# Attention plus quantised feed-forward layer on eight cores: the P·V products of a head pair issued after the fourth score block, two quantisation steps moved into the loop, and one absolute-maximum reduction per group in place of two

## The reference

```python
x = L0_attn_x                                   # (8, 2048, 1024), f32
# causal attention, 16 heads of 64, no output projection
ln = _layernorm(x)
q, k, v = ln @ W_query, ln @ W_key, ln @ W_value
weights = softmax(where(causal, q @ k.T, -inf) / sqrt(64))
x = x + weights @ v
# feed-forward with ternary weights and 8-bit activations
def act_quant(x):                               # one scale per token
    scale = 127.0 / clip(max(abs(x), axis=-1), 1e-05)
    return clip(round(x * scale), -128, 127) / scale
def weight_quant(w):                            # one scale per matrix
    scale = 1.0 / clip(mean(abs(w)), 1e-05)
    return clip(round(w * scale), -1, 1) / scale
h = act_quant(_layernorm(x)) @ weight_quant(w1).T        # 1024 -> 4096
h = silu(depthwise_conv1d(h, conv_w, width 3) + conv_b)
return x + act_quant(h) @ weight_quant(w2).T             # 4096 -> 1024
```

## Time and profile before

| | us |
|---|---|
| median of the runs | 2214.39 |
| the two runs | 2199.25, 2229.52 |
| the profiled execution | 2193.41 |
| its span on the slowest core (core 5), first to last instruction | 2191.9 |
| spans of the eight cores | 2180.6 to 2191.9 |
| DVE busy | 1063.7 |
| TensorE busy | 1093.1 |
| ACT busy | 830.4 |
| GpSimd busy | 280.9 |

### The profile page before, as it was taken

One profiled execution on the slowest core, in us unless ns is written; L12 is line 12 of the kernel. 1 busy time (PEld: TensorE's weight loads), 2 busy tenths in 40 slices (PEclk: granted clock), 3 DMA queues, 4 the chain that ended last, 5 costly groups with the idle time before them and its releaser, 6 DMA issues.

```text
span 2191.9 us, 23798 instructions; the slowest of 8 cores (2180.6 to 2191.9 us)
## 1 busy us (share of the span) xinstructions
PE 1093.1 (50%) x7038; PEld 598.7 (27%) x7038; DVE 1063.7 (49%) x2058; ACT 830.4 (38%) x904; POOL 280.9 (13%) x255
## 2 busy tenths in 40 slices
PE   0577974344554455510424365373473553757465
PEld 0233421122222233200222233232232332434322
DVE  1444343523355555544546446445465464555650
ACT  3100002877755566701332432424413425242422
POOL 0000000000000000000013113113131131322220
PEclk9988985555565566655666687686686877879787
DMA  7310021753343464357322223203222232132300
GB/s 233 96 39 20 1 77 38 237 205 132 138 139 121 138 199 131 129 168 227 113 68 77 70 66 125 68 33 112 74 71 87 68 121 62 58 126 67 116 20 19
DMA packets 108273, 224.03 MB, mean 102 GB/s; under 512 B 4593, under 2 KB 70258, under 8 KB 104050
## 3 DMA queue, kind: packets, MB, share of 16 engines
q1 hardware_dynamic: 94962, 172.18, 24.5%
q0 software_dynamic: 13184, 50.34, 6.5%
HBM read 188.94 MB, written 33.55 MB: 102 GB/s over the span
## 4 chain that ended last, share of the span: by engine, by line
DVE 30%; PE 24%; DMA 17%; ACT 15%; issue 9%; DVEq 1%; POOL 1%; SPq 1%; ACTq 0%; POOLq 0%
PE psO L75 10%; PE psQK L75 7%; DMA wbuf<-w1t 6%; DVE t1s L75 5%; DVE hsil L75 4%; ACT PT L75 4%; DVE smalls L75 4%; DVE tmpc L75 3%; DVE cbuf L75 3%; DMA wbuf<-w2t 3%; ACT hf L75 3%; DMA x1t<-x1scr 3%; DVE amx L75 3%; ACT hq L75 2%; ACT hsil L75 2%
## 5 line engine op out<-in xcount | busy, mean ns | idle before, releaser
L75 PE MATMUL psM<-xqT,t1b 128*128 128x258 bf16 x2048 | 334.7, 335 | 437.6 <-DVE cbuf L75 430.8
L75 PEld LDWEIGHTS psM<-xqT,t1b 128*128 128x128 bf16 x2048 | 237.7, 120 | 533.7 <-issue 465.1
L75 ACT ACTIVATE PT<-psS,smalls 128x1024 bf16<-128x1024 f32 (+1 forms) x320 | 316.0, 987 | 174.2 <-PE psS L75 146.7
L75 ACT ACTIVATE tmpc<-psM,convb_s,convw_s 128x256 f32<-128x256 f32 x256 | 145.0, 567 | 442.2 <-PE psM L75 237.5
L75 PE MATMUL psS<-qT,kT 64*128 64x512 bf16 x640 | 171.9, 544 | 216.4 <-ACT PT L75 216.3
L75 PE MATMUL psO<-t2T,hq 128*128 128x512 bf16 x1024 | 223.9, 381 | 35.4 <-ACT hq L75 35.4
L75 POOL TENSOR_TENSOR hsil<-cbuf,hsil 128x1024 f32<-128x1024 f32 x64 | 150.6, 2353 | 614.9 <-ACT hsil L75 614.9
L75 DVE SCALAR_TENSOR_TENSOR tmpc<-psM,convw_s,tmpc 128x256 f32<-128x256 f32 x256 | 123.7, 483 | 217.6 <-ACT tmpc L75 195.6
L75 ACT ACT_TABLE_LOAD x26 | 33.4, 1283 | 341.3 <-DVE smalls L75 170.8
L75 PE MATMUL psPV<-vaug,PT 128*128 128x65 bf16 x2176 | 113.4, 233 | 65.4 <-DVE PT L75 65.4
L75 PEld LDWEIGHTS psO<-t2T,hq 128*128 128x128 bf16 x1024 | 100.0, 98 | 157.9 <-issue 39.8
(11 more groups left out here) (82 smaller groups left out, 1155.0 us busy)
## 6 DMA issues: line engine op xcount, KB each, us to landing
t1b<-t1scr SPq DMA_DIRECT2D x64, 1024.0 KB, 5.3
wbuf<-w1t SPq DMA_DIRECT2D x32, 1024.0 KB, 6.4
wbuf<-w2t SPq DMA_DIRECT2D x32, 1024.0 KB, 6.2
xstage<-x POOLq DMA_DIRECT2D x16, 512.0 KB, 4.0
x1st<-x POOLq DMA_DIRECT2D x4, 2048.0 KB, 11.0
x1scr<-x1st POOLq DMA_DIRECT2D x4, 2048.0 KB, 9.3
t1scr<-t1s SPq DMA_DIRECT2D x16, 512.0 KB, 3.4
t2scr<-t1s SPq DMA_DIRECT2D x16, 512.0 KB, 3.2
```

Source lines behind the costliest of these rows:

```text
L75: inst = getattr(self.raw, name)(*a, **kw)
```

## The change

Three things are changed, none of them in what is computed.

1. `flush_pv` is called after the scores of kc == 3 in every block, not after kc == 5 in the blocks t = 1, 2 and 3.
2. The head pairs (3, 0) and (3, 4) take three weight steps instead of two. All 66 steps then stand within the loop, and the last two stand ahead of the last `flush_pv` instead of behind it.
3. `amaxpA` goes. `emit_Bamax` waits for all eight `silu` and reduces the 32 blocks in one instruction into `amx`; the reduction into `psNb` and the maximum of the two halves go.

```diff
-                        if kc == (3 if t == 0 else 5):
+                        if kc == 3:
                             flush_pv()
...
-                    emit_wsteps(2)
+                    emit_wsteps(3 if (t == 3 and hp in (0, 4)) else 2)
...
-                            if e == 3:
-                                @sec_v
-                                def _(ve, g=g):
-                                    for hq_ in (3, 7, 11, 15):
-                                        VE.wait(toks[("silu", g, hq_)])
-                                    if g >= 1:
-                                        VE.wait(toks[("amtr", g - 1)])
-                                        VE.wait(toks[("s2col", g - 1)])
-                                    srcA = hsil[:, 0:16 * GRP].rearrange(
-                                        "p (c s) -> p s c", c=16)
-                                    toks[("amaxpA", g)] = VE.emit(
-                                        "tensor_reduce", amx[:], srcA,
-                                        AX.X, ALU.max,
-                                        apply_absolute_value=True)
...
             def emit_Bamax(g):
                 @sec_v
                 def _(ve, g=g):
-                    for hh in (19, 23, 27, 31):
+                    for hh in (3, 7, 11, 15, 19, 23, 27, 31):
                         VE.wait(toks[("silu", g, hh)])
-                    VE.wait(toks[("amaxpA", g)])
-                    srcB = hsil[:, 16 * GRP:32 * GRP].rearrange(
-                        "p (c s) -> p s c", c=16)
-                    VE.emit("tensor_reduce", psNb[:, 0:GRP], srcB,
-                            AX.X, ALU.max, apply_absolute_value=True)
+                    src = hsil[:].rearrange("p (c s) -> p s c", c=32)
                     toks[("amaxp", g)] = VE.emit(
-                        "tensor_tensor", amx[:], amx[:], psNb[:, 0:GRP],
-                        ALU.max)
+                        "tensor_reduce", amx[:], src, AX.X, ALU.max,
+                        apply_absolute_value=True)
```

## The result

The changed kernel takes 2144.56 us in the median of its runs, the kernel before 2201.39 beside it. The ratio is 0.9736, with a 95% interval of 0.9702 to 0.977: 57 us or 2.6% faster. I had predicted 2156 and 43 us.

What follows compares the result with a forecast made beforehand. It took a chain passing from engine to engine as the bound (DVE 30%, TensorE 24%), with quantisation pacing t = 2 and 3. Terms -51.4 + 10.4 - 1.8 = -42.8 us gave 2156 us, range 2130 to 2188.

Steps and rivals of the forecast that it cites:

- the cover that was said to hide the products with V: Part 2, t = 3: mask waits for DVE's quantisation 2.0 us past the exponentials, so earlier products cost nothing there.
- The middle reduction goes, 8.93 us per group: Part 3, between blocks 15 and 16: removing the reduction saves 8.93 us per group, 71.4 us over eight groups.
- Rival (b): Part 3, behind the middle reduction: `t1b` or input tiles come late, 28 us lost, 2184 us; chance 0.17.
- The long reduction at 14.1 us: Part 3, group end: one reduction over 8192 elements per partition, 1024 bytes apart, takes 14.1 us.
- Rival (a): Part 3, group end: the long reduction takes only 9.8 us, the sum is -60.5, 2139 us; chance 0.10.
- 20.0 us given back at the end of the groups: Part 3, group ends: longer reduction costs 1.9 us in each of groups 1 to 7, 6.6 in group 0.
- Part 3, -51.4: Part 3 as a whole: 71.4 us saved less 20.0 us given back, a gain of 51.4 us.
- The store of `x1st`, +10.4 us: End of part 2: last epilogue and store stand exposed behind the last quantisation step, 10.4 us later, bounds 9.9 to 13.4.
- Products with V, -1.8: Part 2, t = 1: products beside whole exponentials get 0.22 us more cover per head pair, 1.8 us gained.
- rival (d): Part 2, t = 1 to 3: products with V set the pace, +17 us overall, 2216 us; chance 0.06.
- Moved steps don't shorten the quantisation: Part 2, t = 3: load and DVE chain has no gap for a third step, so it ends at 980.7 as before.
- Rival (c): End of part 2: moved steps shorten the quantisation by 24.2 us, the sum is -67, 2132 us; chance 0.05.

Runs made afterwards that it cites:

- e4: Kernel before without the middle reduction, the end reduction in two halves, the first between the two psO evacuations, the second behind them: 2121.92 us, ratio 0.9647.
- e10: Changed kernel with the long reduction reading hsil as 256 runs of 32 neighbouring elements, so other maxima: ratio 0.9726 to the kernel before.
- the second measurement: The changed kernel itself measured again, beside other runs of the kernel before: 2143.00 against 2193.01 us, ratio 0.977.
- e1: Kernel before with the reductions of part 3 alone changed, one long reduction per group: 2137.73 against 2192.99 us, ratio 0.9721.
- e2: Kernel before with only the products with V issued after kc == 3 for all t: 2192.16 against 2192.99 us, ratio 0.9987.
- e3: Kernel before with only three weight steps at head pairs 0 and 4 of t = 3: 2201.12 against 2192.99 us, ratio 1.0041.
- e5: Kernel before with each quantisation step's load put ahead of the previous step's store on SyncE's queue: 2118.61 against 2193.01 us, ratio 0.966.
- e7: Kernel before with load ahead of store on SyncE's queue, products with V at kc == 3 and the moved weight steps: 2119.63 us, ratio 0.9658.
- e12: Changed kernel with the load ahead of the store on SyncE's queue: 2063.74 us, ratio 0.9395 to the kernel before.
- e8: Kernel before with end reduction in two halves, load ahead of store and products with V at kc == 3, without moved steps: 2046.01 against 2191.74 us, ratio 0.9315.

## Why the prediction was right or wrong

The mechanism was right for each term of the sum, and the sum was low by 7 to 14 us (-42.8 against -50 and -57). Two things were wrong: the cover that was said to hide the products with V, on which no term of the sum rested, and the price of the last store.

- *The middle reduction goes, 8.93 us per group.* Right to 0.01 us in group 2, with the wait of 2.11 us behind it. And it was right in every group, 8.9 us in the mean of the cores. `t1b` was not late: TensorE starts the matmuls of e = 6 where I had said 1401.2, and waits for DVE and not for a load. Rival (b) falls.

```profile
1401.31 4.03 PE L75 MATMUL psM<-xqT,t1b 128*128 128x258 bf16 x20 [4.64 <-DVE cbuf L75]
```

- *The long reduction at 14.1 us.* It took 14.09 in the mean. The contiguous kernel shows that the stride was the right reason, and that the lower bound of 9.8, taken from 1024 contiguous elements, was itself too high: 8.69. (The 11.3 between the bounds was also a slip: at 1220 ns per 1024 elements, 256 results account for 2.1 us of the old 7.0, and the sum is 11.9.) The rule of the Trainium skill that was quoted (Vector Engine (DVE) Microarchitecture Reference, section 5.2) holds in both columns: 1.73 and 1.05 ns per element there, 1.72 and 1.06 here. It settled less than I made of it: its 1.73 is for one of two sources hopping 4 KiB, and the same section has an instruction with one source, alternating between two regions, at the full rate. The row of the old reduction carried the forecast. Rival (a) needed the stride not to matter.
- *20.0 us given back at the end of the groups.* For one group 1.9 was said, 14.85 - 13.16 = 1.7 was measured, and both ways of restoring the cover (e4, e10) brought 11.5 and 11.4 us in groups 1 to 7, where 7 x 1.7 is 11.8. This term was 1.6 us too large, because DVE waited 0.73 us for the transposes and not the 0.98 of group 0. The 6.6 of group 0 was right.
- *Part 3, -51.4.* It was -56.7 after and -55.5 by the same stretches of the second measurement; e1 alone had -55.3 by its times. Groups 1 to 7 gained 52.1 instead of 71.4 x 7/8 - 13.4 = 49.1, of which 1.6 is the term above, and group 0 3.4 to 4.6 instead of 2.3. A part of the rest lies in the load of `x1t`. In group 2 of the core shown it was waited for 0.84 us instead of 2.37 at e = 5. Summed over the groups, in the mean of the cores, the waits for it at e = 5 come to 8.0 to 8.7 us in the five profiled kernels that have the middle reduction (before, e2, e3, e5, e7) and to 5.4 to 6.8 in the four with the one long reduction (after twice, e1, e12). That is about 2 us of the 5.3. At e = 2 these waits did not shrink by more than they scatter (19.0 to 21.3 us against 18.9 to 20.2). I had looked at this load only as something that might become late, and had named a DVE that waits for a load at e = 4 to 7 as a sign of being wrong; such a wait is there, but it was longer before. The rest, some 1.7 us, is not explained.
- *The store of `x1st`, +10.4 us.* The tail grew by 8.8 us (3.2 to 12.0), below my lower bound of 9.9. The store was issued 4.2 us behind the last step, as said (987.45 - 983.22). I had taken 9.3 us for the store, the median of the DMA issues; behind 0.75 of issue GpSimd waited 7.19, 7.94 together. The DMA view shows what one store had for company. First the kernel before from 449 to 462 us, the store that was waited for 11.49 us (queue, kind: packets, MB, share of 16 engines):

```profile
q0 software_dynamic: 528, 2.10, 39.3%
q1 hardware_dynamic: 272, 1.05, 26.9%
issues: line engine op xcount, KB each, median us to landing
x1scr<-x1st POOLq DMA_DIRECT2D x1, 2048.0 KB, 11.3
```

then the kernel after from 987 to 996 us:

```profile
q0 software_dynamic: 528, 2.10, 59.5%
issues: line engine op xcount, KB each, median us to landing
...
x1scr<-x1st POOLq DMA_DIRECT2D x1, 2048.0 KB, 7.8
```

The store of 2.10 MB is queue 0 in both. A weight load of 1.05 MB ran beside it in the first, nothing in the second. But company is only a part of the answer. The store of t = 1, before, had no other transfer of its core beside it either. From its issue to the next instruction of GpSimd it took 8.5 to 9.7 us on the eight cores, 9.1 in the mean; the store with the load took 11.2 to 13.1, and the moved one 7.2 to 8.6, 7.8 in the mean. So the term that was mis-sized is the price of the exposed store, 9.3 us where it took 7.9 on the core shown. The median mixed stores with and without company, yet a row in which the store was alone would have said 8.8 to 9.1. Why the last store is 1.3 us quicker than the one of t = 1 stays open; when it runs, no engine of its core is at work, which no run varied.
- *Products with V, -1.8.* -3.5 and -1.9 in the two measurements, -2.6 alone; the first stretch took 226.5 to 226.9 us in the five profiled kernels without this edit and 223.4 to 225.6 in the seven with it. In t = 2 and 3 nothing, as said, but the cover that I named was not needed: the claim "2.4 us per head pair without that cover" is refuted by e7 and e8, and rival (d) with it. It would not have been slower in any case.
- *Moved steps don't shorten the quantisation.* Right, and for the reason given: with the serial order removed they save 7 to 8 us (e7, e12), with it at most 3. Rival (c) falls.

The measured 2144.56 lies in the range, and on the faster side of the line of 2% on which I had put the forecast; that it is clear of that line in the first measurement owes something to a kernel before that read 8 us higher then than in later ones. By the stretches of the first profile the change brought 56.7 - 4.2 = 52.5 us, 9.7 more than the sum: 5.3 in part 3, 1.6 in the tail, 1.7 in the products with V, 1.1 in the quantisation. The base of 2199.25 was within 2 us of the kernel before in the first measurement and 6 us above it in the second.

## What to carry to other kernels

A partial result that is taken early to shorten the end is worth it only if it stands where its engine waits; at a point that passes from engine to engine it costs its whole length and the wait in front of it, less the wait that would stand there anyway (11.04 - 2.11 us here). Here the same sixteen reductions cost 71 us less when both halves were put into waits that were there already.

A queue on which load i + 1 stands behind a store that waits for the work of step i makes double buffering useless. Its sign in a profile is an engine that waits for a DMA at every step, with the load issued right behind the store; and while it is there, edits elsewhere in that stretch show nothing (e2, e3), which is no proof that they are hidden for the reason one believes.

A transfer that becomes exposed is better priced by the range of its rows than by their median, and the lower end of the range was still too high here. A load that gets more room is a gain to be looked for, as one that gets less is a risk; here it was some 2 us.

## What the runs showed of the hardware that I had not expected

- A reduction of 8192 f32 elements per partition on DVE took 8.69 us with its elements adjacent and 14.09 us at 1024 bytes apart, a ratio of 1.62. From this row and the 1220 ns for 1024 contiguous elements, (8686 - 1220) / 7168 = 1.04 ns per element and an estimated 0.15 us for the instruction itself; the two rows also differ in their results, 256 and 1.
- The same reduction into `amx` took 13.83 us in group 0, where no matrix product ran beside it, and 14.13 in group 2, where one did. The half took 7.00 and 7.22. I had put that down to PSUM as the destination; in e4 the half into `amx` takes 7.22 as well when it stands beside the product. So the destination doesn't make the difference. In group 0 of the changed kernel no instruction of another engine ran beside it, and in group 2 nothing but the product did. The contiguous reduction of e10 was not slowed at all: 8.69 us in group 0 without the product and 8.69 in groups 1 to 7 with it. Only the reduction with the stride lost its 2%; why, no run shows.

```profile
1166.69 13.83 DVE L75 TENSOR_REDUCE amx<-hsil 128x256 f32<-128x8192 f32 x1 [3.92 <-POOL hsil L75]
```

- The store of 2.10 MB from `x1st` took 7.8 us to landing at the end of part 2 and 11.3 beside a load of 1.05 MB, on the two cores shown. Alone at t = 1 it took 8.2, so the load accounts for most of the difference and not for all of it.
